# Second attention's weights in 25 parts under the first feed-forward layer, stages that overlap at both borders of that attention, and fills and signals spread over the engines

## The reference

```python
x = x + attn_a(layernorm(x))   # first attention
x = x + ffn(layernorm(x))      # first feed-forward layer
x = x + attn_b(layernorm(x))   # second attention
x = x + ffn(layernorm(x))      # second feed-forward layer, same weights
```

```python
kva = x @ wkv_a                       # 64 latent + 64 rotary
ckv = rms_norm(kva[..., :64]) * kv_norm_scale
k_nope, v = split(ckv @ wkv_b)        # per head 128 + 128
scores = (q_nope @ k_nope.T + rope(q_pe) @ rope(k_pe).T) * 192 ** -0.5
out = softmax(causal(scores)) @ v @ wo
```

## Time and profile before

| | before |
|---|---|
| median of 3 runs | 1094.31 us (1091.87 to 1096.7) |
| profiled execution | 1099.08 us, its span 1096.2 us |
| PE busy | 956.0 us (87%) |
| DVE busy | 780.8 us (71%) |
| ACT busy | 536.2 us (49%) |
| POOL busy | 379.0 us (35%) |
| mean granted clock of PE | 0.937 of full speed |
| DMA | 53.69 MB, mean 49 GB/s |

### The profile page before, as it was taken

One profiled execution on the slowest core, in us unless ns is written; L12 is line 12 of the kernel. 1 busy time (PEld: TensorE's weight loads), 2 busy tenths in 40 slices (PEclk: granted clock), 3 DMA queues, 4 the chain that ended last, 5 costly groups with the idle time before them and its releaser, 6 DMA issues.

```text
span 1096.2 us, 20238 instructions
## 1 busy us (share of the span) xinstructions
PE 956.0 (87%) x6656; PEld 753.6 (69%) x6656; DVE 780.8 (71%) x2502; ACT 536.2 (49%) x1379; POOL 379.0 (35%) x476
## 2 busy tenths in 40 slices
PE   1578999988889999467899999999999996899997
PEld 1567878877766666255678787787878775766663
DVE  5866688878889987124576767676677664998983
ACT  1114455554445455311466657575656671255455
POOL 3436688885634433302110111201110100234335
PEclk9767799998999999858899999999999997899999
DMA  5443244443222332330000000000000002333330
GB/s 192 78 78 71 60 84 81 79 87 56 55 55 63 72 65 51 109 128 0 1 1 1 1 1 1 1 1 2 1 1 1 1 1 49 83 75 80 74 85 31
DMA packets 57478, 53.69 MB, mean 49 GB/s; under 512 B 6288, under 2 KB 55840, under 8 KB 57248
## 3 DMA queue, kind: packets, MB, share of 16 engines
q1 hardware_dynamic: 57376, 52.41, 21.4%
HBM read 34.30 MB, written 17.30 MB: 47 GB/s over the span
## 4 chain that ended last, share of the span: by engine, by line
PE 59%; DVE 25%; issue 8%; DMA 3%; POOL 2%; ACT 2%; SPq 0%; POOLq 0%; DVEq 0%; ACTq 0%
PE bank L248 17%; PE bank L1699 7%; PE bank L1647 4%; DVE arena L1076 4%; PE bank L1635 4%; PE bank L1707 4%; PE bank L1479 3%; PE bank L1491 2%; PE bank L1688 2%; DVE xn L282 2%; PE bank L1476 2%; PE bank L1295 2%; PE bank L1309 2%; DMA arena<-b_wo 2%; PE bank L1517 1%
## 5 line engine op out<-in xcount | busy, mean ns | idle before, releaser
L1076 DVE TENSOR_REDUCE arena<-bank 128x2 f32<-128x512 f32 (+1 forms) x192 | 129.0, 680 | 25.8 <-PE bank L1479 25.4
L736 ACT ACTIVATE weights<-bank 128x512 f32<-128x512 f32 x144 | 85.6, 596 | 103.4 <-PE bank L1491 102.3
L809 ACT ACTIVATE weights<-weights,neg_max 128x128 f32<-128x128 f32 (+1 forms) x256 | 113.6, 447 | 31.7 <-DVE neg_max L1236 31.7
L1699 PE MATMUL bank<-kbT,arena 128*128 128x128 f32 (+1 forms) x512 | 112.2, 342 | 2.9 <-DVE neg_max L1236 2.9
L611 POOL TENSOR_SCALAR_AFFINE_SELECT weights<-weights 128x256 f32<-128x256 f32 x144 | 66.5, 463 | 137.5 <-ACT weights L736 137.4
L1479 PE MATMUL bank<-kf_stack,q_stack 96*128 96x128 f32 (+1 forms) x512 | 111.7, 322 | 0.0
L574 POOL TENSOR_SCALAR weights<-weights 128x512 f32<-128x512 f32 x64 | 95.6, 1502 | 22.8 <-ACT weights L668 22.8
L1236 DVE CUSTOM_DVE_ANT_0 weights<-bank,arena 128x128 f32<-128x128 f32 (+1 forms) x256 | 80.3, 351 | 15.0 <-PE bank L1699 14.5
L816 ACT ACTIVATE weights<-bank 128x384 f32<-128x384 f32 x128 | 62.6, 489 | 52.0 <-PE bank L1707 51.8
L1246 DVE TENSOR_SCALAR weights<-weights,inv_sum 128x128 f32<-128x128 f32 (+1 forms) x256 | 84.2, 371 | 4.6
L1699 PEld LDWEIGHTS bank<-kbT,arena 128*128 128x128 f32 x512 | 72.4, 192 | 17.0 <-issue 13.6
(11 more groups left out here) (217 smaller groups left out, 2604.9 us busy)
## 6 DMA issues: line engine op xcount, KB each, us to landing
q_stack<-scr_q SPq DMA_DIRECT2D x144, 128.0 KB, 3.8
scr_q<-q_hi SPq DMA_DIRECT2D x24, 256.0 KB, 2.3
scr_q<-q_lo SPq DMA_DIRECT2D x24, 256.0 KB, 2.5
ka_stack<-scr_k SPq DMA_DIRECT2D x48, 76.5 KB, 3.9
x_all<-x SPq DMA_DIRECT2D x8, 256.0 KB, 6.1
arena<-b_wqn SPq DMA_DIRECT2D x1, 2048.0 KB, 8.1
arena<-b_wo SPq DMA_DIRECT2D x1, 2048.0 KB, 17.0
out<-x_all SPq DMA_DIRECT2D x8, 256.0 KB, 2.3
```

Of the source, the lines that this page charges most:

```text
L736: a.activation(pT[(STEPS * b + k) % N_PT], p2[k % 2][:, :], ACT.Exp).then_inc(s["exp"], 1)
L809: last = a.activation(p, p, ACT.Exp, scale=-1.0, bias=neg_max[:, h % 4, t:t + 1], accum_out=sums[:, h % 4, t:t + 1])
L1076: v.tensor_reduce(into, p1[k % 2][:, :].rearrange("p (h k) -> p h k", h=n), AX.X, ALU.max, negate=True).then_inc(s["maxed"], 1)
L1699: last = mm(ps_s[h % 2][:, t * P:t * P + (t + 1) * P], qT[b % 2][:, h, t * P:(t + 1) * P], kbT[b % 2][:, 0:(t + 1) * P], start=True, stop= ...
```

## The change

Four parts.

1. The weights of the second attention come in 25 pieces (`pieces()`), which SP issues in the odd steps of the feed-forward batches 3 to 6. For that they get places that the first two layers don't use at that time: `st_wo` has its own tile, the second feed-forward layer's working room lies at another offset of the arena, `qT0` and `qT1` are exchanged, and a scratch operand of the attention's rotation (`rope2`) lies in `q_lo`.
2. The stages overlap at both borders. The products of the weights go beside the steps of feed-forward batch 7 (`weights_b(k)`), the preparation of the attention's batch 0 beside the steps of the tail (`beside_f`), and the first 24 steps of the second feed-forward layer beside the 16 heads of the attention's last batch (`steps_beside_b`, 24 steps on 16 heads). The waits of the engines for the last `x_done` at either border are gone, replaced by narrower ones.
3. The shared keys of the feed-forward layers are written by POOL in step 8 (`keys_of_f`), unscaled; ACT's copy to `kf_stack` applies the scale.
4. The 125 signals are issued by PE, ACT and SP, a stage each (`begin`); the zero fills are on DVE; two other small fills and a split of weights stand a few steps earlier or later.

The diff, cut to its core ("@@" names the engine's block):

```diff
-N_FILLS, N_DVE_FILLS = 8, 15
+N_FILLS, N_DVE_FILLS, N_STAGED = 7, 15, 25
...
+        st_wo = sb("st_wo", [P, H, D], f32, scope_c)
...
-        st_wqn, st_wo, st_wk, st_wv, st_pe = cut((H, D), (H, D), (H, LORA), (H, LORA), (NC, W_ABS + H * ROPE))
-        qT0, qT1, q_tok, mask_b = cut((H, T), (H, T), (NT, H, P), (2 * P,))
+        sa.update(nm=nm, nm_row=nm_row)
+        sf[0].update(room(0))
+        sf[1].update(room(2 * H * T))
+        _, st_wqn, st_wk, st_wv, st_pe = cut((H * T,), (H, D), (H, LORA), (H, LORA), (NC, W_ABS + H * ROPE))
+        qT1, qT0, q_tok, mask_b = cut((H, T), (H, T), (NT, H, P), (2 * P,))
         qT = [qT0, qT1]
-        rope2 = y
+        rope2 = q_lo[:, :, :].bitcast(f32)
...
+        def beside_f(b, k, weights_b, step_b):
+            if b == B - 1:
+                weights_b(k)
+            elif b >= B and (b - B) * STEPS + k + 1 < H:
+                step_b(0, 0, (b - B) * STEPS + k + 1)
+
+        def steps_beside_b(h):
+            return [(n // STEPS - 2, n % STEPS) for n in range(3 * h // 2, 3 * (h + 1) // 2)]
...
+        def begin(eng, s):
+            for name, n in s["per"].items():
+                if n:
+                    eng.sem_inc(s[name], n)
...
@@ SP
+            begin(sp, sm)
...
+            def pieces():
+                for h in range(0, H, 8):
+                    yield st_wv[:, h:h + 8, :], b_wvT[:, h:h + 8, :]
+                for h in range(0, H, 2):
+                    yield st_wo[:, h:h + 2, :], b_wo.rearrange("(h p) n -> p h n", p=P)[:, h:h + 2, :]
...
             for s, b, k in steps_af():
                 (step_a if s is sa else step_f)(b, k)
-            sp.wait_ge(*at(sf[0], "x_done", B - 1, 1))
-            sp.dma_start(st_wqn, b_wqn).then_inc(s_stage, 16)
...
-            sp.dma_start(st_wo, b_wo.rearrange("(h p) n -> p h n", p=P)).then_inc(s_stage, 16)
-            sp.wait_ge(*at(sm, "x_done", B - 1, 1))
+                if s is not sa and 3 <= b < B - 1 and k % 2 == 1:
+                    if (b, k) == (3, 1):
+                        sp.wait_ge(*at(sa, "x_done", B - 1, 1))
+                    for into, source in itertools.islice(piece, 1 + (b == 3 and k == 1)):
+                        sp.dma_start(into, source).then_inc(s_stage, 16)
...
@@ POOL
-            for s in (sa, sf[0], sm):
-                for name, n in s["per"].items():
-                    if n:
-                        pool.sem_inc(s[name], n)
-            def fill_stacks(i):
-                g.memset(q_stack[i][0:STK, :, :].bitcast(f32), 0.0).then_inc(s_fill, 1)
-                g.memset(ka_stack[i][0:STK, :, :].bitcast(f32), 0.0).then_inc(s_fill, 1)
...
+                def keys_of_f(b):
+                    kv_sh = s["gate_room"][-1]
+                    pool.wait_ge(*at(s, "k_sel", b, 3))
+                    pool.wait_ge(*at(s, "kT_ps", b, 0))
+                    g.tensor_copy(k48[:, :, 0:HD], kv_sh).then_inc(s["k48"], 1)
+                    pool.wait_ge(*at(s, "k48", b, 1))
+                    g.tensor_tensor(k48[:, :, HD:2 * HD], kv_sh, k48[:, :, 0:HD].bitcast(f32),
+                                    ALU.subtract).then_inc(s["k48"], 1)
+                    g.tensor_copy(k48[:, :, 2 * HD:3 * HD], k48[:, :, 0:HD].bitcast(f32)).then_inc(s["k48"], 1)
...
                 def step(b, k):
                     if k == 3 and there(b + 2):
                         pool_rstd(s, b + 2)
+                    if k == 8 and there(b + 1):
+                        keys_of_f(b + 1)
...
@@ ACT
+            begin(act, sf[0])
...
                     if k == 11 and there(b + 1):
...
-                                     ACT.Copy).then_inc(s["k_stack"], 1)
+                                     ACT.Copy, scale=HD ** -0.5).then_inc(s["k_stack"], 1)
...
@@ DVE
+            def fill_stacks(i):
+                v.memset(q_stack[i][0:STK, :, :].bitcast(f32), 0.0).then_inc(s_fill, 1)
+                v.memset(ka_stack[i][0:STK, :, :].bitcast(f32), 0.0).then_inc(s_fill, 1)
...
-            fill_values()
+            fill_stacks(0)
...
-                if (b, k) == (-2, 13):
+                if (b, k) == (-2, 9):
                     split_a(2 * D, 4 * D, 1)
+                if (b, k) == (-2, 14):
+                    fill_values()
...
-                if (b, k) == (-1, 2):
+                if (b, k) == (-1, 4):
+                    fill_stacks(1)
                     fill_shifts()
...
-                        dve.wait_ge(*at(s, "kT_ps", b, 0))
-                        link(s, "k48", b, 1, v.tensor_scalar(k48[:, :, 0:HD], kv_sh, scale, None, ALU.mult))
...
+            def weights_b(k):
+                if k in range(1, 5):
+                    i = k - 1
+                    dve.wait_ge(b_prep, k)
+                    v.tensor_copy(m_vo[:, 2 * i:2 * i + 2, :], halves((ps_a, ps_b)[i % 2])).then_inc(b_mvo, 1)
+                if k in range(5, 9):
+                    i = k - 5
+                    low_b(i, (i // 2, slice(W_ABS + (i % 2) * 512, W_ABS + (i % 2 + 1) * 512)),
+                          (ps_a, ps_b)[i % 2][:, :], 3 + i)
+                if k == 9:
+                    low_b(4, (slice(0, NC), slice(0, W_ABS)), st_pe[:, :, 0:W_ABS], 2)
+                    low_b(5, (slice(0, NC), slice(W_PE, W_COLS)), st_pe[:, :, W_ABS:], 2)
+                    dve_stats(sm, 0)
...
+                if k == 11:
+                    dve_normalize(sm, 0)
...
@@ PE
+            begin(pe, sa)
...
+            def weights_b(k):
+                if k > 7:
+                    return
+                if k == 0:
+                    pe.wait_ge(s_stage, 16 * N_STAGED)
...
+                elif k > 1:
+                    pe.wait_ge(*((b_mvo, k - 1) if k < 6 else (b_lo, k - 5)))
+                bank, i = (ps_a, ps_b)[k % 2], k % 4
...
-            for h in range(H):
-                step_b(0, 0, h)
+            for s, b, k in steps_af():
+                (step_a if s is sa else step_f)(b, k)
+                if s is not sa:
+                    beside_f(b, k, weights_b, step_b)
+            pe.wait_ge(*at(sf[0], "y", B - 1, 6))
+            pe.wait_ge(*at(sf[0], "oT", B - 1, 2))
...
+                    if b == B - 1:
+                        for n in steps_beside_b(h):
+                            step_g(*n)
             attend_b(B - 1, H // 2 - 1)
             project_b(B - 1, H // 2 - 1)
-            pe.wait_ge(*at(sm, "x_done", B - 1, 1))
-            step_f = ffn(sf[1])
-            for b, k in steps_f():
-                step_f(b, k)
+            for b in range(B + 2):
+                for k in range(STEPS):
+                    step_g(b, k)
```

298 lines of the change are left out of this document (164 added, 134 removed).

## The result

The changed kernel takes 1037.28 us, the median of 4 runs (1034.72 to 1040.56); its time over the kernel before is 0.9495 (95% interval 0.9455 to 0.9536). The forecast was 1028.3 with a range of 1012 to 1046. The profiled execution's span fell from 1096.2 to 1038.8 us, 57.4 us where 66 were forecast. PE does as much as before in less time: 937.6 us busy (90%) at a mean granted clock of 0.955.

The account below looks back on a forecast made before the run. PE, in order and nearly full except at the start and two border dips, was taken as the bound. Savings of 46 - 1 + 13 + 5 + 3 = 66 us off the 1094.3 us median gave 1028.3, range 1012 to 1046.

Parts of the forecast that it names:

- the 61 us of the first border: Last batch's first scores to the second attention's first turned probabilities: 61 us forecast, 107 before.
- First border: First feed-forward layer to second attention: overlapping the stages saves 46 us, ends 28 and 50.
- The products of the weights: Beside feed-forward batch 7: half their former PE time at full clock, 9.6 us.
- DVE's work of step 9 and the statistics: Feed-forward batch 7: low parts of staged weights and statistics on DVE make PE wait 2 us.
- rival A: Clock stays lower beside both borders, which give only 28 and 4 us: 1055 us; chance 0.15 shared with another rival.
- Second border: Second attention to last feed-forward layer: 24 preparation steps beside batch 7's heads save 13 us, ends 4 and 17.
- the choice of the expert: On DVE beside heads 12 and 13 of the attention's last batch: delays PE by 3.5 us.
- Keys: Feed-forward layers: moving the shared keys from DVE to POOL saves 5 us, ends 8 saved and 2 lost.
- The discount of 1.5 us: Keys on POOL: DVE operations with two SBUF inputs wait for POOL, saving 1.5 us less, 0.12 us in each of 13 batches.
- Transfers: 25 weight pieces under feed-forward batches 3 to 6: cost 1 us, ends 0 and 6.
- Rival C: Weight transfers delay q_stack loads in batches 3 to 6, every step waits: 1108 us at 20 us a batch; chance 0.03.
- Start: Program start: fills on DVE and spread signals save 3 us net, ends 9 saved and 3 lost.

Follow-up runs that it names:

- 4: Changed kernel with low parts of the staged weights, statistics and normalisation earlier in feed-forward batch 7: 0.9493 of the kernel before.
- 6: Changed kernel with the attention's batch 0 prepared alone behind the first feed-forward layer's tail: 0.9539 of the kernel before.
- 5: Changed kernel with the 24 steps that prepare the last layer run alone behind the attention's last batch, as before: 0.9649 of the kernel before.
- 1: Changed kernel with the shared keys of the feed-forward layers back on DVE in step 9: 0.9611 of the kernel before.
- 7: Changed kernel with six large weight transfers in place of 25 pieces: 0.9582 of the kernel before.
- 8: Changed kernel with all 25 weight pieces issued in feed-forward batch 6: 0.9613 of the kernel before.
- 2: Changed kernel with both pairs of zero fills back on POOL at their former places, signals still spread: 0.9476 of the kernel before.
- 11: Changed kernel with zero fills back on POOL and low parts of the staged weights and attention's first statistics early in batch 7: 0.9394 of the kernel before.
- 9: Changed kernel with the zero fills on ACT, signals as in the changed kernel: 0.9382 of the kernel before.

## Why the prediction was right, and where it was off

The direction, the mechanisms at both borders and the range held; the time was 9 us later than the likeliest value. That it was not later still is in part luck: the first border and the start fell some 15 us short, and the keys and the second border, forecast too low, gave 5 of them back. Of the signs that the prediction names, the first scores right behind the attention's last product, batch 7 of the attention (36.4 us, near 40 forecast) and the shorter period (19.19 us, 19.4) came; the 61 us of the first border were 70.9, with a clock of 0.50 for 6.7 us of them. By its steps:

- **First border, 46 forecast, 36 measured.** The term of the sum that was mis-sized. PE was to be busy for 53.0 us and idle for 8.1, and was busy for 60.0 and idle for 10.9. Four parts make 9.3 of these 10 us. The products of the weights took 12.1 us for 9.6, since the forecast halved the 19.1 us, where the granted clock of their stretch, 0.63, gives 12.1 (2.5 us). DVE's work of step 9 and the statistics left a hole of 3.7 us for the assumed 2, since PE, being in order, had nothing of batch 0 to do until its x was normalised (1.7 us). Behind that hole the clock was at 0.50 and 0.86 for 13.5 us of PE work, where the forecast had full speed; at 1.00 the same work is some 9.2 us (4.3 us, an estimate from these rows; rival A, which came true for this stretch alone of the two borders). And PE waited 0.8 us for the last piece of the weights. Moving DVE's work ahead (4) took the hole away and gave 3 us. That the preparation hides little beside the tail was in the range: alone it costs 6.7 us more (6).
- **Second border, 13 forecast, 14.3 measured** by undoing it (5). The size is right by two errors against each other: the choice of the expert was priced at 3.5 us and cost at most 0.6, and the clock of batch 0 gave 1.7 us for 3.
- **Keys, 5 forecast, 7.7 to 8.7 measured** (1, and the table). DVE ends the half batch at full weight; that PE is nearly as full took nothing off. The discount of 1.5 us (0.12 us a batch) that the prediction works out by the Trainium skill's section Who interferes with whom (SBUF — State Buffer) had the wrong sign. The wait of DVE's product beside POOL's sum was there before the change, and the move took it away (1).
- **Transfers, 1 forecast, 1 measured** (7, 8): the 0.8 us that PE waited for the last piece. The queues' share was higher than forecast, 0.70 for 0.55, so the margin was smaller. Rival C, the starved stacks, is what happens with large or crowded transfers, at 3 to 6 us a wait and not at a whole batch.
- **Start, 3 saved forecast, nothing or a loss of 2 measured**, inside the ends of -3 and 9. The step that failed is that the 5.7 us of the second pair and the stall that it replaces would balance: with both shift rows, 2.19 us each, and the gaps between the fills it made a block of 11.7 us ahead of the query rotations, and from 20 to 60 us PE had a granted clock of 0.69 for 0.79 before. Undoing the fills (2, 11) and moving them to ACT (9) give 9 to 12 us: the fills were the one part of the change that cost time. With the fills on POOL as before the change the start is 320.7 and 322.9 us, against 331.5 before. So the rest of the fourth part, the signals and the small moves, is worth some 10 us by difference; no run undoes it alone.

## What to carry to other kernels

Take a long stretch of transfers off a border in pieces small enough that no other load waits behind one, and spread them so that the queues stay below full; the same bytes cost 10 us when large or crowded. When stages of in-order engines are laid beside each other, look at what the busiest engine waits for first in the new stage, and let the slower helpers do that several steps ahead. Long fills belong to an engine that nobody waits for then: here both POOL and ACT did better than DVE, though DVE was idle for much of that time. When a forecast takes the time of the same products at a higher clock, it should scale by the clock in the row and not by a half.

## What the runs showed of the hardware

- A DVE `tensor_scalar` of operands in SBUF beside POOL's two large fills took 6.05 and 6.66 us instead of 0.74 and 1.04, so it is held for both fills; a fill of the same size on ACT (3.60 us for 96 x 4096 numbers, 3.47 on DVE, 3.51 on POOL) held no DVE operation beside it. It goes the other way too: beside DVE's low parts of the weights (2.64 us, both inputs in SBUF) POOL's causal mask of 128 x 512 numbers took 2.73 us, 0.63 otherwise.
- Signals at the begin of a program are not equally cheap: POOL's 125 were done by 10.9 us and ACT's 36 by 3.2 us, while PE's 59 alone held it until 10.1.
- The same start code gave 328.7 to 334.1 us in six profiled executions: in a stretch where PE waits much, one profile can't tell 3 us.
